# A cross-attention and two-expert feed-forward kernel: the search for the largest expert weights moved from attention into shared-stage tiles 0 to 7, the split of the weights into tiles 8 to 15

## The chip, the cores and the metric

The kernel runs on one core of a Trainium2 chip. The metric is the device time of one execution in microseconds, lower is better. A core has TensorE (PE, matrix products), VectorE (DVE), ScalarE (ACT), GpSimd (POOL) and a queue of its own for loads and stores (SP), which run side by side and wait for one another on semaphores.

## The reference

```python
def reference(x, ctx, tgt_mask, src_mask, ...):          # x 4x1024x512, ctx 4x64x512
    x = x + xattn(layernorm(x), ctx, ...)                # 16 heads of 64, 64 keys, two masks
    return x + ffn(layernorm(x), ...)
def ffn(x, gate_w, w1, b1, w2, b2, sw1, sb1, sw2, sb2):
    top1 = argmax(softmax(xf @ gate_w.T))                # one of two experts for each row
    masked = xf[None] * one_hot(top1).T[:, :, None]      # rows of the other expert are zero
    h = relu(einsum('end,edh->enh', masked, w1) + b1)    # 512 -> 2048
    routing = (einsum('enh,ehd->end', h, w2) + b2).sum(0)
    shared = relu(xf @ sw1 + sb1) @ sw2 + sb2
    return routing + shared
```

A row that an expert isn't given still gets the expert's constant, relu(b1) @ w2 + b2.

## The kernel before

Products are made from float32 in three float16 parts: high times high, high times low, low times high. Each operand is first scaled by a power of two that comes from the largest magnitudes of the weights, and then split into a high half (ScalarE, `eh`) and a low half (VectorE, `el`). So the largest magnitude of a matrix must be known before its first split.

Three stages follow one another, each ended by a barrier of all engines.

**Attention** works on 32 tiles of 128 rows, one an iteration. Each engine has its order written out in `body(g)`: `step(eng, g, u, d, fn)` calls `fn` for the tile `d` ahead of the iteration's. TensorE does transposes (L429, L450), scores (L440) and the output (L461). GpSimd does the two `rstd` chains (L624 to L630), `norm` (L641), `lo_x` (L649), `add_bo` (L645), `sub` (L636) and `low_w` (L658). VectorE does `residual` (L721, L724), `lo_p` (L689), the mask and the statistics (L731, L695), `sums` (L711, L713), the aggregates (L701, L707), `masked` (L737, L742), `gate` (L754), then `largest_w` (L747 twice, L751), and `pick` (L761). `largest_w` reads 128 rows of 512 of `w1` and of `w2` (`ew`, loaded by L377 and L378) and keeps the running maximum `amw`.

**The shared stage** runs all 4096 rows through the shared network: 16 tiles of 256 rows, each in 16 steps `j` over the hidden width. TensorE does `first(j)` (L978, 12 matmuls into `pH`) and then `second(j-2)` (L990, 6 matmuls into `pY`). ScalarE makes the relu twice (L1009, L1011), VectorE takes the low half, `lo_h(j)` (L1024, semaphore `hl`). `second(j)` waits for `hl` of step j, so VectorE's instruction behind a wait holds TensorE up two steps later. At j=3 stands `result` of the tile before (L1032), to which GpSimd adds the bias (L1179), at j=6 four one-hots (L1327, L1328), at j=11 the next tile's `z` (L1017).

Beside this the expert weights go through the core: `load_e` (L1147) fills `er[u]` with 256 rows of `w1` and of `w2` for each tile, `split_hi` and `split_lo` stand at j = 12 and 14 (`BF = 12`), `idle_expert` at j=13 adds relu(b1) times the rows of `w2` to `cacc` (L1366), and `store_e` (L1152, L1153) writes the halves to `e_split`. Before the first split come the maximum over partitions on GpSimd (L1173) and 18 linked steps on VectorE, `expert_scales`, at j=4 of tile 0 (L151 to L172). At tile 1, j=3, VectorE makes `slots()`, a long linked chain for the order of the rows. SP's queue is in order: at the start of the stage it loads the second `z` tile, three quarters of the shared weights, the bias row, then the first x1 rows and the first `er`.

**The expert stage** takes the rows in the order of their experts, 17 tiles, with the split weights read back (L1409, L1410).

`groups(eng, n, body)` writes the iterations -1, 0, 1 and the last ones out and puts the others in a loop of the engine.

## Time and profile before

| | us |
|---|---|
| median of 3 runs (1948.7 to 1955.52) | 1953.84 |
| the profiled execution | 1952.96 |
| its span in the trace | 1951.2 |
| TensorE busy (matmul) | 1881.4 |
| VectorE busy | 855.0 |
| ScalarE busy | 849.4 |
| GpSimd busy | 523.9 |

Attention lasts to about 516 us of the span, the shared stage from 521 to 1220, the expert stage from 1222 to the end. Busy time is an average over stages. What a change is worth is read from the waits: an engine's idle time counts only where TensorE, or the loop that sets an iteration's length, waits for it.

### The profile page before, as it was taken

Reading aid. Unit: us, or ns where it says so; the run is one execution under the profiler, and the core shown is the slowest. Engines: PE = TensorE matmul, PEld = TensorE weight load, DVE = VectorE, ACT = ScalarE, POOL = GpSimd, SP = SyncE. Lnnn points to the kernel's source line nnn. Section 1 sums busy time; section 2 is a strip of 40 time slices with the busy share of each in tenths; the row PEclk is TensorE's granted clock in tenths of the full one; section 3 lists DMA queues with packets and bytes.
Section 4 is the critical chain, followed back from the end, with each engine's and each line's share of the span. In section 5 each row is a group of like instructions: output and inputs, shape, how many; then the busy total and the mean of one; then the engine's idle time right before and its main releaser. Section 6 shows DMA issues by size and latency. Waiting matters only on the chain. (4 is left out here: it accounts for less than half of the span.)

```text
span 1951.2 us, 35601 instructions
## 1 busy us (share of the span) xinstructions
PE 1881.4 (96%) x11964; PEld 1197.9 (61%) x11965; DVE 855.0 (44%) x1669; ACT 849.4 (44%) x1506; POOL 523.9 (27%) x635
## 2 busy tenths in 40 slices
PE   8889999999799999999999999999999999999997
PEld 6344444444466666666666666666666666666664
DVE  6988787778543333333333333222222222222222
ACT  4654444444344444444444443344443343444333
POOL 1068888888300000000000001121221111222111
PEclk9999999999899999999999999999999999999998
DMA  8245555554652222232322261611111010111100
GB/s 318 78 144 176 166 165 167 164 169 153 228 197 77 76 76 76 79 104 75 109 85 75 75 238 65 227 40 38 38 51 33 27 32 29 43 32 47 40 18 15
DMA packets 123587, 197.32 MB, mean 101 GB/s; under 512 B 20208, under 2 KB 61680, under 8 KB 123120
## 3 DMA queue, kind: packets, MB, share of 16 engines
q1 hardware_dynamic: 115584, 171.01, 26.3%
q0 software_dynamic: 7920, 25.17, 4.0%
q8 instruction: 56, 0.92, 0.2%
q14 instruction: 27, 0.22, 0.0%
HBM read 137.95 MB, written 58.98 MB: 101 GB/s over the span
## 5 line engine op out<-in xcount | busy, mean ns | idle before, releaser
L978 PE MATMUL pH<-room_a,room_w 128*128 128x256 f16 (+1 forms) x6336 | 768.6, 272 | 8.2 <-PEq L335 5.3
L990 PE MATMUL pY<-room_w,room_a 128*128 128x512 f16 (+1 forms) x3120 | 757.8, 380 | 4.6 <-DVE room_a L1024 4.6
L978 PEld LDWEIGHTS pH<-room_a,room_w 128*128 (+1 forms) x6336 | 612.1, 98 | 187.8 <-issue 22.0
L1024 DVE TENSOR_TENSOR room_a<-room_a 128x256 f16<-128x256 f32 (+1 forms) x528 | 233.8, 443 | 888.3 <-ACT room_a L1011 888.2
L990 PEld LDWEIGHTS pY<-room_w,room_a 128*128 128x128 f16 x3120 | 305.2, 98 | 264.5 <-DVE room_a L1024 4.9
L1009 ACT ACTIVATE room_a<-pH,e_bsel,sc 128x256 f32<-128x256 f32 (+1 forms) x272 | 151.8, 558 | 406.0 <-PE pH L978 389.7
L1009 ACT ACTIVATE room_a<-pH,b1s,sc 128x256 f32<-128x256 f32 x256 | 144.5, 565 | 365.1 <-PE pH L978 364.4
L1179 POOL TENSOR_TENSOR room_a<-room_a,s_brow 128x512 f32<-128x512 f32 x32 | 42.4, 1348 | 616.6 <-DVE room_a L1032 616.6
L461 PE MATMUL pO<-room_w,room_b 128*128 (+1 forms) x768 | 171.8, 380 | 2.7 <-DVE room_b L689 2.7
L1011 ACT ACTIVATE room_a<-pH,e_bsel,sc 128x256 f16<-128x256 f32 (+1 forms) x272 | 149.6, 550 | 0.0
L1423 POOL DMA_INDIRECT rows_room<-z_scratch,e_iz x33 | 33.7, 1021 | 415.3 <-DVE e_iz L1416 410.1
L1011 ACT ACTIVATE room_a<-pH,b1s,sc 128x256 f16<-128x256 f32 x256 | 142.4, 556 | 0.0
L461 PEld LDWEIGHTS pO<-room_w,room_b 128*128 128x128 f16 x768 | 75.3, 98 | 87.2 <-DVE room_b L689 2.9
L440 PE MATMUL pS<-room_w,room_a 128*128 (+1 forms) x384 | 87.3, 385 | 5.3 <-POOL room_a L649 5.3
L440 PE MATMUL banks_a<-room_w,room_a 128*128 (+1 forms) x384 | 85.6, 379 | 5.4 <-POOL room_a L649 5.2
L1468 POOL TENSOR_TENSOR room_a<-room_a,e_sel 128x512 f32<-128x512 f32 x33 | 43.8, 1347 | 147.8 <-DVE room_a L1032 147.8
L534 ACT ACTIVATE room_b<-room_b,shift,rs 128x512 f32<-128x512 f32 x32 | 26.0, 813 | 117.1 <-POOL shift L630 117.1
L641 POOL TENSOR_TENSOR room_b<-room_b 128x1024 f32<-128x1024 f32 x32 | 71.6, 2237 | 0.0
L440 PEld LDWEIGHTS pS<-room_w,room_a 128*128 128x128 f16 x384 | 37.7, 99 | 50.4 <-issue 7.4
L1017 DVE SCALAR_TENSOR_TENSOR room_a<-banks_a,room_a 128x512 f16<-128x512 f32 x65 | 41.9, 686 | 60.1 <-ACT room_a L999 60.1
L440 PEld LDWEIGHTS banks_a<-room_w,room_a 128*128 128x128 f16 x384 | 37.1, 98 | 50.2 <-issue 4.5
L636 POOL TENSOR_TENSOR room_b<-room_b 128x1024 f32<-128x1024 f32 x32 | 61.3, 1916 | 1.0 <-DVE room_b L742 1.0
(184 smaller groups left out, 1546.7 us busy)
## 6 DMA issues: line engine op xcount, KB each, us to landing
room_b<-in_w SPq DMA_DIRECT2D x64, 256.0 KB, 4.5
s_er<-in_w SPq DMA_DIRECT2D x32, 512.0 KB, 6.3
room_w<-e_split SPq DMA_DIRECT2D x8, 2048.0 KB, 16.8
rows_room<-in_x SPq DMA_DIRECT2D x32, 256.0 KB, 4.6
room_a<-in_sw SPq DMA_DIRECT2D x32, 256.0 KB, 5.0
room_b<-in_x SPq DMA_DIRECT2D x32, 256.0 KB, 2.8
s_split<-room_a SPq DMA_DIRECT2D x64, 128.0 KB, 4.2
x_scratch<-room_b SPq DMA_DIRECT2D x32, 256.0 KB, 3.1
```

Source lines behind the costliest of these rows:

```text
L440: mm = e.matmul(pS[u % 2][:, h * 512:(h + 1) * 512], xt[:, u % 2, k, :], f[:, k, bass.ds(b, 1), h * 512:(h + 1) * 512], start=(n == 0), st ...
L461: mm = e.matmul(pO[:, :], pt[:, q, :], f[:, bass.ds(b, 1), q, :], start=(n == 0), stop=(n == 3 * PAIRS - 1))
L636: e.tensor_tensor(v, v, mx[:, u % 2, :].unsqueeze(2).broadcast_to([P, HEADS, KEYS]), ALU.subtract).then_inc(S["sub"], 1)
L641: e.tensor_tensor(v, v, ri[:, u % 2, :].unsqueeze(2).broadcast_to([P, HEADS, KEYS]), ALU.mult).then_inc(S["prob"], 1)
L978: mm = q.matmul(self.pH[j % 2][:, 0:rows], w[:, k, j * P:(j + 1) * P], zt[:, u, k, 0:rows], start=(n == 0), stop=(n == 3 * KC - 1))
L990: mm = q.matmul(self.pY[u][r][:, :], h[:, j % self.HR, r * P:(r + 1) * P], w[:, j, :], start=(j == 0 and n == 0), stop=(j == HC - 1 and n ...
L1009: q.activation(self.hf[:, j % self.HR, 0:rows], self.pH[j % 2][:, 0:rows], ACT.Relu, bias=b, scale=self.a1)
L1011: q.activation(self.hh[:, j % self.HR, 0:rows], self.pH[j % 2][:, 0:rows], ACT.Relu, bias=b, scale=self.a1).then_inc(self.S["hh"], 1)
L1017: v = q.scalar_tensor_tensor(out=self.zTl[:, u, :, r * P:(r + 1) * P], in0=self.pZ[:, r, :].rearrange("p (k n) -> p k n", k=KC), scalar=LN ...
L1024: q.tensor_tensor(self.hl[:, j % self.HR, 0:rows], self.hf[:, j % self.HR, 0:rows], self.hh[:, j % self.HR, 0:rows], ALU.subtract).then_in ...
L1179: v = q.tensor_tensor(net.ob[:, u, r, :], net.ob[:, u, r, :], brow[:, :], ALU.add)
L1468: v = q.tensor_tensor(net.ob[:, u, r, :], net.ob[:, u, r, :], sel[:, u, :], ALU.add)
```

## The change

In attention, `largest_w`, its two loads an iteration, its buffers and `amw` go.

The shared stage goes over the expert weights twice, in 16 steps each. In tiles 0 to 7, steps 0 to 15, two a tile: VectorE at j=5 and j=12 waits for the load and does `idle_expert`, and in the two `j` behind each takes the largest magnitude of the two halves of `er` (`largest`, one reduce of 1024 elements each, into `seen`). After the last `j` of tile 7 it takes the maximum of `seen`. GpSimd's reduction over partitions and the 18 steps of `expert_scales` move from tile 0 to tile 8 (the latter at j=4 as before). In tiles 8 to 15 the weights are loaded again and split, two steps a tile, at j = 5 and 7 and at j = 12 and 14. SP's order is written anew for this; expert 0's weights are still read back before tile 14's work. SP, GpSimd, ScalarE and VectorE have the stage's iterations all written out (`unrolled`); TensorE keeps its loop and its order. The expert weights are still read from memory twice: 64 loads of 0.25 MB go from attention, and 32 loads of 0.5 MB more stand in the shared stage.

```diff
+def unrolled(n, body):
+    for g in range(-1, n + 1):
+        body(g)
...
-                        def largest_w(e, g, u):
-                            e.wait_ge(S["ew_in", u % 2], 2 * dma_count2(g, u))
-                            for c in range(2):
-                                e.tensor_reduce(ewm[:, u % 2, c:c + 1], ew[:, u % 2, c, :], AX.X, ALU.max,
-                                                apply_absolute_value=True).then_inc(S["ew_max"], 1)
-                            e.wait_ge(S["ew_max"], 2 * count(g, u))
-                            at_least(e, S["amw"], count(g, u) - 1)
-                            e.tensor_tensor(amw[:, 0:2], amw[:, 0:2], ewm[:, u % 2, :], ALU.max).then_inc(S["amw"], 1)
...
-                            at_least(e, S["ew_max"], 2 * count(g, u) - 4)
-                            e.dma_start(ew[:, u % 2, 0, :], rows(units(w1), g, u)).then_inc(S["ew_in", u % 2], 16)
...
-                                step(dve, g, u, 2, largest_w)
...
+        PASS = TILES // 2
+        AT = (5, 12)
...
+                def load_e(q):
+                    if 2 <= q < TILES + 2:
+                        sp.wait_ge(S["seen"], 2 * (q - 1))
+                        sp.wait_ge(S["cacc"], 2 * (q - 1) + 1)
+                    if q >= TILES + 2:
+                        sp.wait_ge(S["el"], 2 * (q - TILES - 1))
+                    for i, w in enumerate((w1, w2)):
+                        sp.dma_start(er[:, q % 2, i, :, :], net.rows(units(w), q % TILES)).then_inc(S[f"e_in{q % 2}"], 16)
+                def store_e(q):
+                    n = q - TILES
+                    sp.wait_ge(S["el"], 2 * n + 2)
+                    for i, d in enumerate((e1_d, e2_d)):
+                        sp.dma_start(net.rows(units(d[0]), n), eh[:, i, :, :]).then_inc(S["e_out"], 16)
...
+                load_z(1)
...
+                load_r(0)
+                load_e(0)
+                for t in range(TILES):
+                    if t > PASS:
+                        store_e(2 * t - 1)
+                    load_e(2 * t + 1)
+                    if t == TILES - 2:
+                        sp.wait_ge(S["e_out"], 64 * TILES // 2)
                         load_set(nc, sp, wB, e1_d, e2_d, 0, w_in)
-                    for u in range(N):
-                        if not isinstance(g, int) or g >= 0:
-                            step(sp, g, u, 2, load_z)
-                        step(sp, g, u, 1, load_r)
-                        step(sp, g, u, 1, load_e)
-                        step(sp, g, u, -1, store)
-                        step(sp, g, u, 0, store_e)
-                groups(sp, TILES // N, body)
+                    if t + 2 < TILES:
+                        load_z(t + 2)
+                    if t + 1 < TILES:
+                        load_r(t + 1)
+                    if t > 0:
+                        store(t - 1)
+                    if t >= PASS:
+                        store_e(2 * t)
+                    if t + 1 < TILES:
+                        load_e(2 * t + 2)
+                store_e(2 * TILES - 1)
+                store(TILES - 1)
...
+                        if N * g + u == PASS:
+                            pool.wait_ge(S["e_am"], 2)
+                            pool.partition_all_reduce(sc[:, ARE:ARE + 3], sc[:, AME:AME + 3], P, RMAX).then_inc(S["e_red"], 1)
...
+                def split_hi(n, i):
+                    act.wait_ge(S[f"e_in{n % 2}"], 16 * TILES + 32 * (n // 2 + 1))
+                    at_least(act, S["e_out"], 64 * n)
+                    act.activation(eh[:, i, :, :], er[:, n % 2, i, :, :], ACT.Copy, scale=sc[:, (EW1, EW2)[i]:(EW1, EW2)[i] + 1]).then_inc(S["eh"], 1)
...
+                            for h, at in enumerate(AT):
+                                if j in (at, at + 2) and PASS <= N * g + u < TILES:
+                                    if N * g + u == PASS and j == AT[0]:
+                                        act.wait_ge(S["e_step"], EXP_STEPS)
+                                    split_hi(2 * (N * g + u - PASS) + h, (j - at) // 2)
...
+                def split_lo(n, i):
+                    dve.wait_ge(S["eh"], 2 * n + i + 1)
+                    dve.scalar_tensor_tensor(out=el[:, i, :, :], in0=er[:, n % 2, i, :, :], scalar=sc[:, (EW1, EW2)[i]:(EW1, EW2)[i] + 1],
+                                             in1=eh[:, i, :, :], op0=ALU.mult, op1=ALU.subtract).then_inc(S["el"], 1)
+                def idle_expert(n):
+                    dve.wait_ge(S[f"e_in{n % 2}"], 32 * (n // 2 + 1))
                     for c in range(2):
-                        q.wait_ge(S["cacc"], 2 * t + c + 1)
-                        e = bass.ds(t // (TILES // 2), 1)
-                        v = cacc[:, e, :].rearrange("p e n -> p (e n)")
-                        q.scalar_tensor_tensor(out=v, in0=er[:, u, 1, c, :], scalar=rb1[:, bass.ds(2 * t + c, 1)], in1=v,
-                                               op0=ALU.mult, op1=ALU.add).then_inc(S["cacc"], 1)
+                        dve.wait_ge(S["cacc"], 2 * n + c + 1)
+                        v = cacc[:, n // PASS, :]
+                        dve.scalar_tensor_tensor(out=v, in0=er[:, n % 2, 1, c, :], scalar=rb1[:, 2 * n + c:2 * n + c + 1], in1=v,
+                                                 op0=ALU.mult, op1=ALU.add).then_inc(S["cacc"], 1)
+                def largest(n, i):
+                    dve.tensor_reduce(seen[:, i, n:n + 1], er[:, n % 2, i, :, :].rearrange("p r n -> p (r n)"), AX.X, ALU.max,
+                                      apply_absolute_value=True).then_inc(S["seen"], 1)
+                def largest_all():
+                    dve.wait_ge(S["seen"], 2 * TILES)
+                    dve.tensor_reduce(sc[:, AME:AME + 2], seen[:, :, :], AX.X, ALU.max).then_inc(S["e_am"], 1)
...
-                            if j == 4 and isinstance(g, int) and g == 0 and u == 0:
+                            if j == 4 and N * g + u == PASS:
...
-                            if j in (BF, BF + 2):
-                                step(dve, g, u, 0, split_lo, (j - BF) // 2)
-                            if j == BF + 1:
-                                step(dve, g, u, 0, idle_expert)
-                dve.tensor_copy(sc[:, AME:AME + 2], amw[:, 0:2])
...
-                groups(dve, TILES // N, body)
+                unrolled(TILES // N, body)
```

VectorE's queue in an iteration of attention, before. The names are buffer<-buffers; L754 is `gate`, L747 and L751 are `largest_w`, L761 `pick`, L721 and L724 `residual`:

```order
L737 SCALAR_TENSOR_TENSOR room_b<-banks_a,sc,room_a 128x1024 [waits a_sim,a_neg]
L742 TENSOR_REDUCE room_b<-room_b 128x16 [waits a_smask]
L754 SCALAR_TENSOR_TENSOR room_a,gg<-room_b,mv,room_a 128x512 [waits a_agg2]
L747 TENSOR_REDUCE room_b<-room_b 128x1 [waits a_ew_in0]
L747 TENSOR_REDUCE room_b<-room_b 128x1
L751 TENSOR_TENSOR amw<-amw,room_b 128x2 [waits a_amw,a_ew_max]
L761 TENSOR_SCALAR expert<-gg,rs 128x1 [waits a_rs2,a_gd]
L721 SCALAR_TENSOR_TENSOR room_b<-pO,sc,room_b 128x512 [waits a_x1_out0,a_z_out0,a_xr_bo,a_att]
L724 BN_STATS st<-room_b 128x6 [waits a_x1]
```

and after, where `gate` is L745 and `pick` L752:

```order
L737 SCALAR_TENSOR_TENSOR room_b<-banks_a,sc,room_a 128x1024 [waits a_sim,a_neg]
L742 TENSOR_REDUCE room_b<-room_b 128x16 [waits a_smask]
L745 SCALAR_TENSOR_TENSOR room_a,gg<-room_b,mv,room_a 128x512 [waits a_agg2]
L752 TENSOR_SCALAR expert<-gg,rs 128x1 [waits a_rs2,a_gd]
L721 SCALAR_TENSOR_TENSOR room_b<-pO,sc,room_b 128x512 [waits a_x1_out0,a_z_out0,a_xr_bo,a_att]
L724 BN_STATS st<-room_b 128x6 [waits a_x1]
```

Nothing else moved; `pick` and `residual` follow `gate` directly.

VectorE's queue at the start of the shared stage, before. L1398 to L1400 stand ahead of tile 0, L1024 is `lo_h`, and with L163 the scales begin:

```order
L1399 TENSOR_SCALAR s_rb<-b1e 128x32
L1400 TENSOR_REDUCE sc<-b1e 128x1
L1024 TENSOR_TENSOR room_a<-room_a 128x256 [waits s_hh,s_rb1]
L1024 TENSOR_TENSOR room_a<-room_a 128x256 [waits s_hh] x4
L163 COPY sc<-sc 128x1 [waits s_e_red]
L151 TENSOR_SCALAR sc<-sc 128x1 [waits s_e_step]
L152 TENSOR_SCALAR sc<-sc 128x1 [waits s_e_step]
L153 TENSOR_SCALAR sc<-sc 128x1 [waits s_e_step]
```

and after, where `lo_h` is L1013, `idle_expert` L1368 and `largest` L1372:

```order
L1414 TENSOR_SCALAR s_rb<-b1e 128x32
L1415 TENSOR_REDUCE sc<-b1e 128x1
L1013 TENSOR_TENSOR room_a<-room_a 128x256 [waits s_hh,s_rb1]
L1013 TENSOR_TENSOR room_a<-room_a 128x256 [waits s_hh] x5
L1368 SCALAR_TENSOR_TENSOR cacc<-s_er,s_rb,cacc 128x512 [waits s_cacc,s_e_in0]
L1368 SCALAR_TENSOR_TENSOR cacc<-s_er,s_rb,cacc 128x512 [waits s_cacc]
L1013 TENSOR_TENSOR room_a<-room_a 128x256 [waits s_hh]
L1372 TENSOR_REDUCE s_seen<-s_er 128x1
```

The scales are gone from here, and the first wait on a load of expert weights (`s_e_in0`) stands behind `lo_h` of j=5.

SP's queue there, before. `room_w<-s_split` are the shared weights, `s_er` the expert weights, `e_split` the stores of their halves:

```order
L1058 DMA room_w<-s_split 128x4x512 x2
L1061 DMA room_w<-s_split 128x4x512 x2
L1137 DMA room_a<-x_scratch 128x2x512 [waits a_x1_out1,a_z_out1,a_z_out0,a_x1_out0]
L1147 DMA s_er<-in_w 128x2x512 x2
L1133 DMA rows_room<-z_scratch 128x2x512 [waits s_zT]
L1137 DMA room_a<-x_scratch 128x2x512
L1147 DMA s_er<-in_w 128x2x512 x2
L1152 DMA e_split<-s_eh 128x2x512 [waits s_el]
L1153 DMA e_split<-s_el 128x2x512
```

and after:

```order
L1047 DMA room_w<-s_split 128x4x512 x2
L1050 DMA room_w<-s_split 128x4x512 x2
L1118 DMA room_a<-x_scratch 128x2x512 [waits a_x1_out1,a_z_out1,a_z_out0,a_x1_out0]
L1132 DMA s_er<-in_w 128x2x512 x4
L1114 DMA rows_room<-z_scratch 128x2x512 [waits s_zT]
L1118 DMA room_a<-x_scratch 128x2x512
L1132 DMA s_er<-in_w 128x2x512 [waits s_cacc,s_seen]
L1132 DMA s_er<-in_w 128x2x512
```

The first load of `er` keeps its place behind the shared weights and the first x1 rows, and the second now follows it at once.

## Rows read from the trace of the kernel before

**Rows 1.** windows of before: stretch, busy us of each engine (instructions), granted clock, DMA

```profile
159.56:485.62 326.06, 313.39 (x1564) 156.37 (x1563) 261.42 (x441) 152.96 (x208) 264.08 (x362) 1.00 0.54 167
...
521.09:564.50 43.41, 43.41 (x298) 30.12 (x299) 15.73 (x43) 19.49 (x36) 1.26 (x3) 0.96 0.73 258
564.50:607.50 43.00, 38.42 (x254) 25.50 (x251) 17.70 (x57) 15.84 (x30) 2.50 (x2) 0.92 0.25 82
```

**Rows 2.** timeline of one attention iteration: start, length, engine, line, [idle before, releaser]

```profile
311.47 0.75 DVE L721 SCALAR_TENSOR_TENSOR room_b<-pO,sc,room_b 128x512 f32<-128x512 f32 x1 [2.47 <-POOL room_b L645]
...
313.03 1.16 POOL L658 TENSOR_TENSOR room_a<-room_a 128x512 f16<-128x512 f32 x1
...
316.37 0.14 DVE L707 BATCH_NORM_AGGREGATE mv<-st 128x2 f32<-128x6 f32 x1
...
318.85 0.74 DVE L754 SCALAR_TENSOR_TENSOR room_a<-room_b,mv,room_a 128x512 f32<-128x512 f32 x1
318.89 2.46 POOL L641 TENSOR_TENSOR room_b<-room_b 128x1024 f32<-128x1024 f32 x1
...
320.83 0.54 DVE L751 TENSOR_TENSOR amw<-amw,room_b 128x2 f32<-128x2 f32 x1
...
321.32 1.15 POOL L649 TENSOR_TENSOR room_a<-room_a 128x512 f16<-128x512 f32 x1
...
322.43 1.27 POOL L645 TENSOR_TENSOR room_b<-room_b,room_a 128x512 f32<-128x512 f32 x1
...
324.00 0.75 DVE L721 SCALAR_TENSOR_TENSOR room_b<-pO,sc,room_b 128x512 f32<-128x512 f32 x1 [2.51 <-POOL room_b L645]
```

**Rows 3.** groups on VectorE, 159 to 480 us: count, busy, mean ns, idle before

```profile
L747 DVE TENSOR_REDUCE room_b<-room_b 128x1 f32<-128x512 f32 x50 | 31.8, 678 | 0.0
...
L721 DVE SCALAR_TENSOR_TENSOR room_b<-pO,sc,room_b 128x512 f32<-128x512 f32 x26 | 19.5, 751 | 61.2 <-POOL room_b L645 35.8 <-issue 25.3
...
L751 DVE TENSOR_TENSOR amw<-amw,room_b 128x2 f32<-128x2 f32 x25 | 14.8, 592 | 0.9
```

**Rows 4.** timeline, TensorE, early attention: the scores of two iterations

```profile
136.22 5.34 PE L440 MATMUL pS<-room_w,room_a 128*128 128x512 f16 x24
...
147.89 5.34 PE L440 MATMUL banks_a<-room_w,room_a 128*128 128x512 f16 x24
```

**Rows 5.** timeline, end of attention: ScalarE, VectorE and GpSimd

```profile
491.12 1.90 POOL L641 TENSOR_TENSOR room_b<-room_b 128x1024 f32<-128x1024 f32 x1
...
496.63 1.02 ACT L522 ACTIVATE room_b<-pP 128x1024 f16<-128x1024 f32 x1 [4.60 <-PE pP L450]
...
498.00 1.21 DVE L689 SCALAR_TENSOR_TENSOR room_b<-pP,room_b 128x1024 f16<-128x1024 f32 x1
```

**Rows 6.** SP's timeline, and issue to landing of its first two `er` loads

```profile
539.34 0.97 SPq L1147 DMA_DIRECT2D s_er<-in_w  x2
...
DMA to landing us min/median/max: 7.0/7.6/8.3
```

**Rows 7.** timeline, tile 0: last of the scale steps, and TensorE's second product j=6

```profile
536.99 0.24 DVE L172 TENSOR_SCALAR b1e_s<-b1e,sc 128x32 f32<-128x32 f32 x1
...
542.49 1.46 PE L990 MATMUL pY<-room_w,room_a 128*128 128x512 f16 x6
```

**Rows 8.** timeline, TensorE, tile 1: the pause and what follows

```profile
585.10 2.74 PE L990 MATMUL pY<-room_w,room_a 128*128 128x512 f16 x6 [4.58 <-DVE room_a L1024]
...
589.98 1.46 PE L990 MATMUL pY<-room_w,room_a 128*128 128x512 f16 x6
```

**Rows 9.** durations: timeline rows of tile 0, and two groups of the whole span

```profile
532.93 0.39 POOL L1173 PARTITION_ALL_REDUCE sc<-sc  x1 [10.97 <-issue]
...
558.51 1.53 DVE L1366 SCALAR_TENSOR_TENSOR cacc<-s_er,s_rb,cacc 128x512 f32<-128x512 f32 x2
...
L770 DVE TENSOR_REDUCE seen<-room_w 128x1 f32<-128x1024 f32 x16 | 19.3, 1209 | 0.0
...
L1328 DVE TENSOR_SCALAR s_hota<-lane,s_place,row_id 128x33 f32<-128x33 f32 x32 | 9.5, 297 | 0.0
```

85 lines of the change are left out of this document (30 added, 55 removed).

## The prediction

> **What bounds the kernel now.** I read it stage by stage. The windows come first [rows 1]: in the 26 attention iterations from 159.56 to 485.62 us TensorE is busy 313.39 of 326.06 us, so it waits about half a microsecond an iteration. In the first shared tile (521.09 to 564.5) it never pauses, 43.41 of 43.41. In the second it pauses 4.58 us. The later shared tiles are like the first. So in the shared stage any other engine's work is free as long as `hl` arrives in time, and everything depends on single waits. In attention, a little could be had.
>
> Then the timeline of one attention iteration [rows 2], to see what sets its length. VectorE adds the residual (L721, 311.47), works without a break to L707 (ends 316.51), and releases GpSimd. GpSimd makes two rstd chains, normalises (L641, 318.89), makes the low part (L649), adds `bo` (L645, ends 323.70) and so releases VectorE's next L721 at 324.00. That loop, 5.0 us on VectorE and 7.2 us on GpSimd with 0.3 us of handing over, is 12.53 us from L721 to L721, and 26 iterations at 12.54 us are the window of [rows 1]. TensorE alone would need 11.67 us: that is the distance of two iterations at the start, before the loop has caught up [rows 4].
>
> **The change, part by part.**
>
> Attention loses `largest_w`: two reduces of 678 ns and a maximum of 592 ns, 1.95 us of VectorE an iteration [rows 3]. They stand after L754 and before L721, that is in VectorE's own time while GpSimd works, not in the loop. In 26 iterations VectorE stood idle 61.2 us before L721, 2.35 each [rows 3]. I expect this idle time to grow to 4.3 us and the iteration to stay at 12.5. The 16.8 MB of loads that go were never waited for. Value taken: 0 for the 26 iterations. At the end of attention there is one place where the three instructions are late work: L689 begins at 498.00, though its input from ScalarE was there at 497.65 [rows 5], so 0.3 us are won; one link of the scales goes at the start, 0.1 us. Term: **-0.4 us**.
>
> The removed maximum has two SBUF inputs and could hold GpSimd. The rows say that it does not: L751 begins at 320.83 and ends with L641 at 321.37, so it waits, and the L649 behind it takes 1.15 us, as L658 does (1.16) with no such instruction beside it [rows 2]. The Trainium skill (SBUF — State Buffer, Who interferes with whom) says that of a VectorE instruction with two SBUF inputs and a GpSimd instruction the one that starts first has the shared ports for its whole length; by that, each of the 25 could have held GpSimd for up to its own length wherever VectorE was first, 25 x 0.59 = 14.8 us to win at most. By the rows here it is nothing.
>
> Tile 0 of the shared stage gains a wait. Before, the first reader of `er` was ScalarE at j=12. Now VectorE waits for `e_in0` at j=5, in `idle_expert`, right behind `lo_h(5)`, with `lo_h(6)` and all later ones queued behind it. Without the 18 steps of the scales, which held it to 537.23 [rows 7], VectorE is there a little earlier still, at about 536.4. But on SP's queue the load of `er` stands behind three quarters of the weights, the bias row and the x1 rows, as before: it is issued at 539.34 in two pieces, which land 7.0 to 8.3 us later [rows 6]. The second goes out at about 539.8, so both are there at 546.8 to 548.1; I take 547.8. Nothing in the change moves this load forward. Behind it come the two multiply-adds, 1.53 us [rows 9], and `lo_h(6)`, 0.43, with 0.15 for hand-overs: `hl(6)` is ready at 549.9. TensorE wants it for the second product at 542.49 [rows 7]. Pause: 549.9 - 542.5 = **+7.4 us** (6.4 to 7.8 by the landings).
>
> After a pause TensorE is slow for a while. The pause of 4.58 us in tile 1 shows the price: one step of six and twelve matmuls took from 585.10 to 589.98, 4.88 us, where 2.60 is usual [rows 8], the granted clock of that stretch being 0.92 [rows 1]. The least is what the six alone lost, 2.74 - 1.46 = 1.3. I take the nearest row whole, **+2.2 us**; a longer pause may cost more, up to one more such step, 4.6.
>
> Tiles 0 to 7: VectorE gets two multiply-adds (1.53 us) and two reduces of 1024 elements (1.21 each [rows 9]) at j=5 to 7 and again at 12 to 14. The worst step is j=6 with the four one-hots (4 x 0.3 [rows 9]): 0.43 + 1.2 + 1.21 = 2.8 us against a step of 2.60, and `hl(j)` is needed two steps after `first(j)`, some 3.5 us after `lo_h` could end. The split of these tiles is gone. 0, in a range to +1. Their loads are issued a tile ahead at j=7 and j=15, with over 20 us to land; SP's order puts no new wait ahead of z, x1 or the stores. 0. Tile 1 keeps the pause of `slots()`, which is unchanged.
>
> Tile 8: the maximum (L1377 in the new file) comes after `lo_h(15)` of tile 7, GpSimd reduces over partitions, and VectorE's 18 steps stand at j=4 of tile 8. That is five steps, 13 us, later. The one such reduction in this stage began 11 us after its operands were there [rows 9] and takes 0.4, so it is in time by about 1.5 us. The 18 steps take at most 3.9 us (533.3, the end of the reduction [rows 9], to 537.23 [rows 7]) and stood at the same j in tile 0 without a pause of TensorE [rows 1]. Here `result` and the bias add of GpSimd stand beside them, which may add 1 us, and the first split follows at once. 0 taken, +2 as the upper end.
>
> Tiles 8 to 15: two steps a tile instead of one, each the pattern that stood at j=12 and 14 and hid completely. Its stores have 12 us until `eh` is written again. At tile 14 they queue behind the 8 MB of expert 0's weights, as no store did at this place before. 0, upper end +2.
>
> Sum, against the profiled execution (1952.96 us, its span 1951.2): 1952.96 - 0.4 + 7.4 + 2.2 = 1962.2. That execution was 0.9 us below the median of the runs, so the forecast is **1963.0 us**. Its own range is 1959 to 1967.
>
> **The rivals.**
>
> Faster. The place is the race in [rows 2]: VectorE's L754 (two SBUF inputs) starts at 318.85, 0.04 us ahead of L641, which then takes 2.46 us; with no such overlap it takes 1.90 (491.12 [rows 5]). L641 is in the loop. If the lighter VectorE queue shifts that order, 0.56 us go in each of some 24 iterations: 13.4 us, and the time is 1963.0 - 13.4 = 1949.6. It decides from a shift of 0.04 us. Against it: nothing that goes stands between L707, which releases both, and L754. The rule of the Trainium skill on that page (who starts first keeps the ports) is what would make such a shift pay. Chance 0.06. The stronger form, that VectorE's queue and not the loop sets the iteration, would bring it to TensorE's 11.67 us: 26 x 0.87 = 22.6 us, 1940.4; the idle 2.35 us before L721 speaks against it. Chance 0.04.
>
> No pause. If the weights landed before 542, or the wait proved harmless, only the -0.4 stays: 1953.4. For it: my landing time rests on two loads. Against: they are issued only at 539.3, and the wait is in VectorE's program order. Chance 0.12.
>
> More pauses. The reduction or the 18 steps are late in tile 8, or the denser splits cost half a microsecond in each of eight tiles: one pause of 2 us with its 2.2 of slow clock, or 8 x 0.5 = 4: 1967 to 1975. For it: the margin at j=5 of tile 8 is of the order of 1 us. Chance 0.13.
>
> The forecast itself has 0.65.
>
> **How the numbers follow.** A measurement of this kernel can tell 0.3%, 5.9 us, from no change; that is 1959.7. The forecast with 0.65 lies above it but for its lower edge, 0.05 (small clock price, early landing); with the more-pauses case, slower is 0.60 + 0.13 = 0.73. Same is 0.05 + 0.12 + half of the first faster case (1949.6 is inside the band), 0.03 = 0.20. Faster is 0.07. The range leaves out the faster cases and the tail of more pauses and takes in the case without a pause: 1953 to 1971.
>
> **What would show it.** Right: in attention L721 still every 12.5 us, with VectorE idle 4.3 us before it; in tile 0 a pause of TensorE near 542 of about 7 us with VectorE's multiply-add on `er` just before its end, released by the load; the shared tiles otherwise at 43 us; at tile 8 no idle TensorE. Wrong: attention's iteration under 12.3 us or L641 at 1.90 throughout; `er` landing before 542; TensorE idle in any of tiles 8 to 15.

## The result, and the profile after

| | before | after |
|---|---|---|
| median of the runs | 1953.88 us (1948.7 to 1955.52) | 1962.63 us (1960.11 to 1967.89) |
| ratio, 95% interval | 1 | 1.0048 (1.0032 to 1.0063) |
| profiled execution: span | 1951.2 us | 1958.4 us |
| first product of the shared stage | 521.09 us | 519.27 us |
| product that opens the expert stage (L1516, now L1531) | 1222.28 us | 1230.45 us |
| length of the shared stage, between the two | 701.19 us | 711.18 us |

The change costs 8.75 us by the medians, 0.4 to 0.5%. The last row says where: the shared stage is 10.0 us longer. Attention ended 1.8 us earlier in this execution, and the expert stage took 1.0 us less (728.9 and 727.95 us from its opening product to the end). Whether these two belong to the change is a question for the runs.

The windows of after, in the stretches of [rows 1] (columns: stretch, then busy us of TensorE, its weight loads, VectorE, ScalarE and GpSimd, granted clock, DMA share, GB/s), and the quiet rest of the stage:

```profile
159.56:485.62 326.06, 312.53 (x1576) 158.51 (x1575) 242.05 (x367) 153.71 (x209) 263.05 (x363) 1.00 0.41 125
521.09:564.50 43.41, 34.83 (x224) 23.05 (x221) 10.02 (x19) 14.33 (x28) 0.00 (x0) 0.86 0.81 269
564.50:607.50 43.00, 38.20 (x258) 25.62 (x257) 23.04 (x63) 13.48 (x27) 2.49 (x2) 0.96 0.27 87
...
607.50:1190.00 582.50, 582.50 (x4073) 400.85 (x4072) 229.57 (x435) 265.55 (x491) 35.20 (x27) 1.00 0.36 123
```

Tile 0, which had no pause before (43.41 of 43.41), has lost 8.58 us. From 607.5 to 1190 us TensorE never pauses: neither the search in tiles 2 to 7, nor the scales in tile 8, nor two splits a tile in tiles 8 to 15 cost anything.

The timeline of after in tile 0, SP's queue, VectorE and TensorE (columns: start us, length us, engine, line, operation; in brackets the idle time before and what ended it). L1132 loads the expert rows, L1368 is the accumulation over the idle expert, L1013 is `lo_h`, L967 and L979 are the first and second products:

```profile
537.89 2.88 SPq L1132 DMA_DIRECT2D s_er<-in_w  x4
547.61 1.54 DVE L1368 SCALAR_TENSOR_TENSOR cacc<-s_er,s_rb,cacc 128x512 f32<-128x512 f32 x2 [12.95 <-DMA s_er<-in_w]
549.07 0.42 DVE L1013 TENSOR_TENSOR room_a<-room_a 128x256 f16<-128x256 f32 x1
549.55 2.74 PE L979 MATMUL pY<-room_w,room_a 128*128 128x512 f16 x6 [8.58 <-DVE room_a L1013]
552.08 2.46 PE L967 MATMUL pH<-room_a,room_w 128*128 128x256 f16 x12
554.37 1.46 PE L979 MATMUL pY<-room_w,room_a 128*128 128x512 f16 x6
```

This is the chain that the prediction drew. VectorE stands 12.95 us for the rows, behind it waits `lo_h(6)`, behind that the second product of j=6. Then one step of eighteen matmuls takes 554.37 - 549.55 = 4.82 us where 2.60 is usual, 2.2 us for the slow clock: the window's granted clock is 0.86, and six matmuls in 2.74 us where 1.46 is usual are near the lower of its two levels, 1.2 of 2.4 GHz.

Tile 8 of after, the scales of the experts (same columns; L1377 is the maximum over the tiles, L1188 the reduction over partitions, L168 and L177 the first and last of the chained steps, L1253 the first split):

```profile
880.08 0.18 DVE L1377 TENSOR_REDUCE sc<-s_seen 128x2 f32<-128x32 f32 x1
880.40 0.39 POOL L1188 PARTITION_ALL_REDUCE sc<-sc  x1 [28.66 <-DVE sc L1377]
893.46 0.14 DVE L168 COPY sc<-sc 128x1 f32<-128x1 f32 x1
896.77 0.24 DVE L177 TENSOR_SCALAR b1e_s<-b1e,sc 128x32 f32<-128x32 f32 x1
897.05 1.15 ACT L1253 ACTIVATE s_eh<-s_er,sc 128x1024 f16<-128x1024 f32 x1 [1.72 <-DVE b1e_s L177]
```

The reduction began 0.1 us after its operands (880.08 + 0.18 to 880.40), and so was ready 12.7 us before it was used. The chain took 3.55 us, and ScalarE waited 1.72 us for it, which nobody felt.

One iteration of attention in after, VectorE and GpSimd, the counterpart of [rows 2] (L745 is `gate`, L754 before; L641 `norm`, L649 `lo_x`, L645 `add_bo`, L721 `residual`):

```profile
319.17 2.48 DVE L745 SCALAR_TENSOR_TENSOR room_a<-room_b,mv,room_a 128x512 f32<-128x512 f32 x1
319.20 1.90 POOL L641 TENSOR_TENSOR room_b<-room_b 128x1024 f32<-128x1024 f32 x1
321.22 1.45 POOL L649 TENSOR_TENSOR room_a<-room_a 128x512 f16<-128x512 f32 x1
322.63 1.27 POOL L645 TENSOR_TENSOR room_b<-room_b,room_a 128x512 f32<-128x512 f32 x1
...
324.20 0.75 DVE L721 SCALAR_TENSOR_TENSOR room_b<-pO,sc,room_b 128x512 f32<-128x512 f32 x1 [2.19 <-POOL room_b L645]
```

This is a surprise. The order of which the faster rival spoke has turned: `gate` starts 0.03 us ahead of `norm`, but is the one that waits (2.48 us where it took 0.74), and `norm` takes 1.90 us where it took 2.46. Yet the iteration is not 0.56 us shorter, only 0.1 (12.39 us from 310.48 to 322.87, where it was 12.50). `gate` ends its work beside `lo_x`, which now takes 1.45 us and not 1.15. From the start of `norm` to the end of `add_bo` it was 4.81 us before (318.89 to 323.70) and is 4.70 now.

So three questions were open. Is tile 0's pause the whole cost? Are the 1.8 us at attention's end a gain of the change? What is the turned order at the port worth?

### The profile page after: what moved, and what is told of

It reads as the page before. It is cut to its first block and busy times, and to the rows that moved or that the text cites. A ratio compares the mean times of both kernels' runs of the same rounds, so it can differ in the third digit from the quotient of the medians.

```text
span 1958.4 us, 34732 instructions
## 1 busy us (share of the span) xinstructions
PE 1880.5 (96%) x11964; PEld 1198.2 (61%) x11965; DVE 861.5 (44%) x1604; ACT 848.2 (43%) x1506; POOL 520.4 (27%) x635
## 5 line engine op out<-in xcount | busy, mean ns | idle before, releaser
L967 PE MATMUL pH<-room_a,room_w 128*128 128x256 f16 (+1 forms) x6336 | 768.8, 272 | 8.3 <-PEq L338 5.3
L979 PE MATMUL pY<-room_w,room_a 128*128 128x512 f16 (+1 forms) x3120 | 758.6, 380 | 13.4 <-DVE room_a L1013 13.4
L967 PEld LDWEIGHTS pH<-room_a,room_w 128*128 (+1 forms) x6336 | 612.4, 98 | 187.7 <-issue 22.6
L1013 DVE TENSOR_TENSOR room_a<-room_a 128x256 f16<-128x256 f32 (+1 forms) x528 | 233.5, 442 | 847.9 <-ACT room_a L1000 842.7
L979 PEld LDWEIGHTS pY<-room_w,room_a 128*128 128x128 f16 x3120 | 305.3, 98 | 273.8 <-DVE room_a L1013 13.9
L461 PE MATMUL pO<-room_w,room_b 128*128 (+1 forms) x768 | 172.7, 382 | 2.6 <-DVE room_b L689 2.6
L461 PEld LDWEIGHTS pO<-room_w,room_b 128*128 128x128 f16 x768 | 75.4, 98 | 87.9 <-DVE room_b L689 3.1
L440 PE MATMUL banks_a<-room_w,room_a 128*128 (+1 forms) x384 | 87.3, 385 | 9.4 <-POOL room_a L649 9.4
L440 PE MATMUL pS<-room_w,room_a 128*128 (+1 forms) x384 | 87.3, 385 | 7.3 <-POOL room_a L649 7.3
L440 PEld LDWEIGHTS banks_a<-room_w,room_a 128*128 128x128 f16 x384 | 37.5, 99 | 55.5 <-issue 8.6
L440 PEld LDWEIGHTS pS<-room_w,room_a 128*128 128x128 f16 x384 | 37.7, 99 | 52.4 <-issue 8.6
L641 POOL TENSOR_TENSOR room_b<-room_b 128x1024 f32<-128x1024 f32 x32 | 63.2, 1976 | 0.0
L721 DVE SCALAR_TENSOR_TENSOR room_b<-pO,sc,room_b 128x512 f32<-128x512 f32 x32 | 24.0, 750 | 86.6 <-POOL room_b L645 78.8
## 6 DMA issues: line engine op xcount, KB each, us to landing
room_w<-e_split SPq DMA_DIRECT2D x8, 2048.0 KB, 18.6
```

Of the source, the lines that this page charges most:

```text
L440: mm = e.matmul(pS[u % 2][:, h * 512:(h + 1) * 512], xt[:, u % 2, k, :], f[:, k, bass.ds(b, 1), h * 512:(h + 1) * 512], start=(n == 0), st ...
L461: mm = e.matmul(pO[:, :], pt[:, q, :], f[:, bass.ds(b, 1), q, :], start=(n == 0), stop=(n == 3 * PAIRS - 1))
L641: e.tensor_tensor(v, v, ri[:, u % 2, :].unsqueeze(2).broadcast_to([P, HEADS, KEYS]), ALU.mult).then_inc(S["prob"], 1)
L967: mm = q.matmul(self.pH[j % 2][:, 0:rows], w[:, k, j * P:(j + 1) * P], zt[:, u, k, 0:rows], start=(n == 0), stop=(n == 3 * KC - 1))
L979: mm = q.matmul(self.pY[u][r][:, :], h[:, j % self.HR, r * P:(r + 1) * P], w[:, j, :], start=(j == 0 and n == 0), stop=(j == HC - 1 and n ...
L1013: q.tensor_tensor(self.hl[:, j % self.HR, 0:rows], self.hf[:, j % self.HR, 0:rows], self.hh[:, j % self.HR, 0:rows], ALU.subtract).then_in ...
```

## The experiments

In all of them the length of the shared stage is measured as in the table above, from its first product to the product that opens the expert stage. It leaves out what attention and the expert stage vary by. Ratios are to the kernel before, run on the same chip in the same rounds. The chips differ: the kernel before took 1950.75 us on that of late_step, early_load, later_load and both_pauses, 1953.54 us on that of attention_only, search_kept, gate_behind and all_three, and 1954.4 us on that of the four repetitions. So an expected time is compared by its ratio.

### Theory and rivals

Theory A: the wait for the expert rows at step 5 of tile 0 makes the whole loss, pause and slow clock. Rival B: the loss lies in the added work of the tiles. If A is right, asking later or loading earlier gives the time back, and loading later costs more.

**late_step.** Tile 0's first search step stands behind step 8 and not step 5:

```diff
+                                    if N * g + u + h == 0:
+                                        at = 8
                                     if j == at:
                                         idle_expert(2 * (N * g + u) + h)
```

> The changed kernel with one edit: in shared-stage tile 0 the first step of the search (the accumulation and the two maxima) stands behind the step 8 in place of step 5 on VectorE; everything else is as changed. Theory A (the pause of tile 0 is what costs): in the changed kernel the accumulation waits until 547.6 us for the expert rows and TensorE stands 8.58 us and then works 2.2 us at the lower clock. Three steps of 1.3 us or more later the pause is gone or is at most 3 us long, and the time falls by 8 to 11 us, from 1962.6 to 1952 to 1955, to about the kernel before. Rival B (the cost is spread over tiles 0 to 15, by the added reductions and the split steps, or lies in the stores): the pause goes and the time stays above 1959. Rival C (the rows are late whenever they are asked for): the accumulation at step 8 still waits more than 5 us and the time stays near 1960.

Measured: 1951.33 us, ratio 1.0004 (0.9995 to 1.0013). The stage took 703.23 us. VectorE and TensorE in its tile 0:

```profile
548.46 1.54 DVE L1368 SCALAR_TENSOR_TENSOR cacc<-s_er,s_rb,cacc 128x512 f32<-128x512 f32 x2 [6.44 <-DMA s_er<-in_w]
550.39 1.47 PE L979 MATMUL pY<-room_w,room_a 128*128 128x512 f16 x6 [2.07 <-DVE room_a L1013]
```

The rows come as late as before, but 7.8 us of TensorE's work (three steps of 2.60) lie ahead of the wait. A pause of 2.07 us is left, and the six matmuls behind it take 1.47 us: no slow clock.

**early_load.** The first pair of expert rows is loaded ahead of the last quarter of the shared weights:

```diff
                 for q in range(1, Q):
+                    if q == Q - 1:
+                        load_e(0)
                     load_quarter(sp, wA, s1_d, s2_d, q, 1, S[f"w1_in{q}"])
...
                 load_r(0)
-                load_e(0)
```

> The changed kernel with one edit: the loads of the first pair of expert rows are issued on SP's queue ahead of the last quarter of the shared weights, at attention's end, and not behind it and the waits for the last stores. Theory A: the rows are there before VectorE's step 5 of tile 0, the 8.58 us pause and its 2.2 us of slow clock go, and the time is 1951 to 1954; the last quarter of the weights lands some 2 to 3 us later and is needed only at step 12 of tile 0, so it costs nothing. Rival B (cost spread over the tiles): above 1959. Rival D (the last quarter comes late in its turn): a new pause in tile 0 at the first matmul of step 12, and 1955 to 1960.

Measured: 1952.1 us, ratio 1.0007 (0.9998 to 1.0016), stage 703.54 us. SP, VectorE and TensorE in its tile 0 (L1369 is the accumulation here):

```profile
530.02 2.37 SPq L1132 DMA_DIRECT2D s_er<-in_w  x2
540.26 1.54 DVE L1369 SCALAR_TENSOR_TENSOR cacc<-s_er,s_rb,cacc 128x512 f32<-128x512 f32 x2 [6.26 <-DMA s_er<-in_w]
542.19 1.47 PE L979 MATMUL pY<-room_w,room_a 128*128 128x512 f16 x6 [1.89 <-DVE room_a L1013]
```

The load goes out 7.9 us earlier and its rows are there 7.3 us earlier. They are still late for step 5, by 1.89 us. The last quarter of the weights was not missed: TensorE has no pause at step 12, the sign of rival D.

**later_load.** The same load, 1 MB later:

```diff
                 load_r(0)
-                load_e(0)
                 for t in range(TILES):
...
+                    if t == 0:
+                        load_z(2)
+                        load_r(1)
+                        load_e(0)
                     load_e(2 * t + 1)
...
```

> The changed kernel with one edit: the first pair of expert rows is loaded behind the z rows of tile 2 and the x1 rows of tile 1 in SP's queue, 1 MB later. Theory A (the pause is as long as the load is late): the pause of 8.58 us grows by the time of 1 MB at the rate of this stretch, about 2.6 us, and the time goes from 1962.6 to about 1965 (1964 to 1967). Rival B (the length of the pause is not what costs): within 1 us of 1962.6.

Measured: 1963.83 us, ratio 1.0067 (1.0053 to 1.0081), stage 714.35 us:

```profile
550.78 1.54 DVE L1371 SCALAR_TENSOR_TENSOR cacc<-s_er,s_rb,cacc 128x512 f32<-128x512 f32 x2 [15.39 <-DMA s_er<-in_w]
552.71 2.74 PE L979 MATMUL pY<-room_w,room_a 128*128 128x512 f16 x6 [11.02 <-DVE room_a L1013]
```

The pause is 11.02 us. Against the three executions with the load unmoved (8.58 above, 7.91 and 9.84 below, mean 8.8) that is 2.2 us more, for a forecast of 2.6. Pause, stage and time move together in all three runs. Theory A stands and rival B has fallen. Rival C was right in one half: at step 8 the accumulation still waited 6.44 us. The time did not stay near 1960 us for that, since the work ahead of the wait covers it.

### Is the gain at attention's end real?

**attention_only.** The kernel before without the search:

```diff
-                            at_least(e, S["ew_max"], 2 * count(g, u) - 4)
-                            e.dma_start(ew[:, u % 2, 0, :], rows(units(w1), g, u)).then_inc(S["ew_in", u % 2], 16)
-                            e.dma_start(ew[:, u % 2, 1, :], rows(units(w2), g, u)).then_inc(S["ew_in", u % 2], 16)
...
-                            link(dve.memset(amw[:, :], 0.0))
+                            link(dve.memset(amw[:, :], 0.1))
...
-                                step(dve, g, u, 2, largest_w)
```

> The kernel before, without the search in attention: its loads of the expert rows (64 in SP's queue) and the step of two maxima and a running maximum are taken out, and the two numbers are a constant 0.1 (the search is left out, so the scales of the expert weights differ; the work of the stages behind does not). The shared stage is that of before. Theory A (as the profile of the changed kernel reads): the attention part is worth 1.8 us to 2.5 us, so 1948.2 to 1949.2 on this chip against 1950.75 of before. Rival as forecast: 0.4 us, so 1950.3. Rival F (the order at the shared port turns and gives the whole 0.56 us to each of the 25 iterations or more): 1937 to 1943.

Measured: 1954.28 us, ratio 1.0002 (0.9993 to 1.0011). Theory A's 1.8 to 2.5 us are refused; the forecast of 0.4 us lies inside the interval, and so does nothing at all. Two groups of its attention, from 160 to 485 us (columns: line, engine, operation, tiles, count, then busy us, mean ns, and idle us before with what ended it; L718 is `residual`, L638 `norm`):

```profile
L718 DVE SCALAR_TENSOR_TENSOR room_b<-pO,sc,room_b 128x512 f32<-128x512 f32 x26 | 19.5, 751 | 104.5 <-POOL room_b L642 104.5
...
L638 POOL TENSOR_TENSOR room_b<-room_b 128x1024 f32<-128x1024 f32 x26 | 60.2, 2315 | 0.0
```

VectorE's idle time before `residual` grew from 61.2 us [rows 3] to 104.5 us, from 2.35 to 4.0 us an iteration. The removed work became waiting, as forecast, and twelve iterations of scores take 150.99 us (311.90 to 462.89) against 150.97 us before (310.17 to 461.14). In this kernel the order at the port has not turned: `norm` takes 2315 ns.

**search_kept.** The changed kernel with the search still in attention, its result unused (the removed loads, `largest_w` and its step put back; shown are the two places that order it):

```diff
                         def load_w(e, g, u):
+                            at_least(e, S["ew_max"], 2 * count(g, u) - 4)
+                            e.dma_start(ew[:, u % 2, 0, :], rows(units(w1), g, u)).then_inc(S["ew_in", u % 2], 16)
+                            e.dma_start(ew[:, u % 2, 1, :], rows(units(w2), g, u)).then_inc(S["ew_in", u % 2], 16)
...
                                 step(dve, g, u, -1, gate)
+                                step(dve, g, u, 2, largest_w)
```

> The changed kernel with the search in attention kept as in before, its result unused: the shared stage is that of the changed kernel, attention that of before. Theory G (the landing of the first expert rows, not attention's end, sets the end of tile 0's pause): attention ends some 1.8 us later, the pause is as much shorter, near 6.8 to 7.4 us, and the time stays that of the changed kernel, within 1 us (ratio to before 1.0048 to 1.0070). Theory H (the rows land as much later as attention ends): the pause stays 8.6 us and the time is 1.8 us above the changed kernel's.

Measured: 1961.8 us, ratio 1.0045 (1.0031 to 1.0059), stage 710.76 us, pause 7.91 us. It is the time of the changed kernel, but it doesn't decide between G and H, since the premise of both failed: with the search kept, the shared stage began at 519.16 us, as early as without it. So the 1.8 us don't come from the search. Nor does the turned order: it stands in this profile too (`gate` 2.48 us beside a `norm` of 1.90 us in two of every four iterations), with the search in place.

**before_again, after_again.** Both kernels unchanged, once more:

> The kernel before, unchanged, once more. Its profiled execution started the shared stage at 521.09 us and the changed kernel's at 519.27 us, while taking the search out of attention alone gave no time (ratio 1.0002) and keeping it gave 519.16 us. Theory L (the start of the stage moves by 1 to 2 us from execution to execution, with where the slow clock falls at attention's end): this profile starts the stage elsewhere than 521.09, between 519 and 523. Theory M (it belongs to the program): 521.1 within 0.3 us. Ratio 1.000 within 0.001.

> The changed kernel, unchanged, once more, on the same chip as the kernels with the pauses taken out. Theory L: the stage starts elsewhere than at 519.27 us, between 519 and 523. Theory M: 519.3 within 0.3 us. The pause of tile 0 is 7.5 to 9 us in either. Ratio to before 1.0048 to 1.0063.

Measured: before 1954.62 us, ratio 1.0001 (0.9992 to 1.001); after 1965.4 us, ratio 1.0054 (1.004 to 1.0068). Before began the shared stage at 522.02 us, after at 522.42 us, 3.1 us later than in its first profile. The end of attention on TensorE in the first profile of after (L461 is the output, L955 the transpose of the first shared rows):

```profile
498.33 7.04 PE L461 MATMUL pO<-room_w,room_b 128*128 128x512 f16 x24 [2.37 <-DVE room_b L689]
...
507.32 1.06 PE L955 MATMUL banks_a<-ident,rows_room 128*128 128x128 f32 x8 [1.07 <-DMA rows_room<-z_scratch]
508.62 5.35 PE L461 MATMUL pO<-room_w,room_b 128*128 128x512 f16 x24 [0.24 <-DVE room_b L689]
519.27 6.07 PE L967 MATMUL pH<-room_a,room_w 128*128 128x256 f16 x36 [5.29 <-PEq L338]
```

and in the second profile of the same kernel:

```profile
499.75 5.35 PE L461 MATMUL pO<-room_w,room_b 128*128 128x512 f16 x24 [2.38 <-DVE room_b L689]
...
509.21 1.91 PE L955 MATMUL banks_a<-ident,rows_room 128*128 128x128 f32 x8 [3.23 <-DMA rows_room<-z_scratch]
510.91 6.22 PE L461 MATMUL pO<-room_w,room_b 128*128 128x512 f16 x24
522.42 5.98 PE L967 MATMUL pH<-room_a,room_w 128*128 128x256 f16 x36 [5.29 <-PEq L338]
```

About 1.7 us of slow clock fall on the last two output products and the transpose between them in both, but at different places. In the first execution the earlier one is slow (7.04 us) and hides in the wait for the shared rows, and the later one runs at full speed (5.35). In the second the earlier is fast, the wait is 3.23 us, and transpose and later product are slow (1.91 and 6.22), in the open. Theory L holds for the changed kernel as far as the start of the stage moves: its two profiles differ by more than the 1.8 us that were to be explained. The kernel before moved by 0.9 us only, with the slow clock in the open both times. What decides where the clock falls, no run tells: the pauses ahead, 2.37 and 2.38 us, are the same. The pause of tile 0, 9.84 us in this second execution, lies above the 7.5 to 9 us that were expected of both.

The place of the slow clock is not all that moved. The order at the port turned in the first profile of after and not in the second, and it can be followed on the scores (L440) from the iteration in which the loop has caught up to the last one, and from there to the first product of the stage:

| | scores, from | to | length | from there to the first product |
|---|---|---|---|---|
| before | 159.56 | 485.19 | 325.63 us | 35.90 us |
| before_again | 160.45 | 486.05 | 325.60 us | 35.97 us |
| after (order turned) | 160.90 | 484.56 | 323.66 us | 34.71 us |
| after_again | 160.28 | 485.98 | 325.70 us | 36.44 us |

Of the 3.1 us between the two executions of after, the turned order has 2.0 and the slow clock 1.7, and the start of the loop takes 0.6 back. The 1.8 us between the first profiles of before and after are 2.0 of the order and 1.2 of the clock, less 1.3 us by which the loop of after began later. Neither can be booked as a gain of the change, since one and the same kernel did it either way. How often each kernel does it, these profiles don't tell.

This pair also gives the cleanest difference, same chip and the same pattern at attention's end: span 1963.2 against 1952.3 us, stage 711.34 against 701.03. The pause of tile 0 in it:

```profile
551.94 1.54 DVE L1368 SCALAR_TENSOR_TENSOR cacc<-s_er,s_rb,cacc 128x512 f32<-128x512 f32 x2 [14.21 <-DMA s_er<-in_w]
...
553.87 2.74 PE L979 MATMUL pY<-room_w,room_a 128*128 128x512 f16 x6 [9.84 <-DVE room_a L1013]
556.40 1.79 PE L967 MATMUL pH<-room_a,room_w 128*128 128x256 f16 x12
558.03 1.46 PE L979 MATMUL pY<-room_w,room_a 128*128 128x512 f16 x6
```

### What is the order at the port worth?

**gate_behind.** In the kernel before, the search's maxima ahead of the gate's product, so that this one can't meet `norm`:

```diff
-                                step(dve, g, u, -1, gate)
                                 step(dve, g, u, 2, largest_w)
+                                step(dve, g, u, -1, gate)
```

> The kernel before with one edit: in attention VectorE does the search's maxima ahead of the gate's product in place of behind it, so that the product no longer starts within 0.05 us of GpSimd's product L641. Nothing is left out. Theory I (the turned order at the port is worth the whole stretch of L641, 2.46 us to 1.90 us, in each iteration): 12.50 us falls to about 11.94 us and the time to 1935 to 1941. Theory J (GpSimd gives the gain back, as in the changed kernel, where L649 went from 1.15 us to 1.45 us and 0.12 us of each iteration was left): 1946 to 1950. Rival K (the product, now late, is itself behind GpSimd and delays the expert's choice): 1950 or slower.

Measured: 1954.19 us, ratio 1.0002 (0.9993 to 1.0011). GpSimd's groups from 160 to 485 us:

```profile
L641 POOL TENSOR_TENSOR room_b<-room_b 128x1024 f32<-128x1024 f32 x26 | 49.5, 1903 | 0.0
L649 POOL TENSOR_TENSOR room_a<-room_a 128x512 f16<-128x512 f32 x26 | 41.1, 1579 | 2.5 <-ACT room_a L517 0.2
```

`norm` fell from 2293 to 1903 ns, `lo_x` rose from 1186 to 1579: what one won, 0.39 us, the other lost. Twelve iterations take 150.90 us against 150.97. Both theory I (0.56 us an iteration) and J's 0.12 us are wrong here; nothing is left. The time is in the range of rival K, but not by its reason: `gate` begins 1.84 us after `norm` and still takes 0.74 us, so it is not held. The collision has only moved from one GpSimd instruction to the next in the same chain.

The shared stage of this kernel, in which nothing was edited, is 1.35 us shorter than before's: about 0.5 us less slow clock at its start, 0.6 us less behind tile 1's pause, and 0.2 us less wait at its end. A difference of that size between two single profiles shows nothing by itself.

### A version that beats both

Tile 1 of both kernels has a pause of its own, 4.58 us before [rows 8] and 4.79 us after: the 35 chained small operations of the slot numbers stand together behind step 3.

**both_pauses**, and again as **two_edits.** The early load, and the slot numbers in pieces of five; `link` now says when a piece is full, and `slots` yields there:

```diff
+                    def link(ins):
+                        issue(ins)
+                        return steps[0] % 5 == 0
...
-                    link(dve.tensor_copy(before, pR[:, 0:SUB]))
+                    if link(dve.tensor_copy(before, pR[:, 0:SUB])):
+                        yield
...
-                            if j == 3 and isinstance(g, int) and g == 0 and u == 1:
-                                slots()
+                            if N * g + u == 0 and j >= 14 or N * g + u == 1 and j < 6:
+                                next(parts, None)
...
```

> The changed kernel with two edits: the early loads as in the kernel before this one, and the 35 chained small operations of the slot numbers, which stood together behind step 3 of tile 1, given in pieces of five behind steps 14 and 15 of tile 0 and 0 to 5 of tile 1. Nothing is left out. Theory A: beside tile 0's pause of 8.58 us and 2.2 us of slow clock, tile 1's pause of 4.6 to 4.8 us and its 2.2 us of slow clock go too; the time is 1943 to 1948, faster than both kernels. Rival E (each piece of about 1.3 us makes VectorE late at its step, seven or eight small pauses): 1949 to 1954, no gain over the early loads alone.

> The kernel with the early loads and the slot numbers in pieces, once more, beside the one with three edits on the same chip. Ratio 0.997 as before.

Measured: 1945.91 us, ratio 0.9975 (0.9966 to 0.9984), stage 694.55 us; again 1947.79 us, ratio 0.9968 (0.9956 to 0.998), stage 694.74 us. The window of tile 1 in two_edits:

```profile
564.50:607.50 43.00, 43.00 (x303) 29.55 (x301) 25.40 (x63) 17.44 (x35) 2.52 (x2) 1.00 0.25 87
```

38.42 busy us at a clock of 0.92 [rows 1] have become 43.00 at 1.00. In tile 0 pauses of 0.82 and 1.28 us are left. This is theory A's range; of rival E's small pauses there is none.

**all_three**, and again as **three_edits.** Both edits, and tile 0's first step behind step 8 as in late_step.

> The changed kernel with three edits: the early loads, the slot numbers in pieces, and the first step of the search in tile 0 behind step 8 in place of step 5. Nothing is left out. With the early loads alone TensorE still stood about 1.7 us in tile 0, since the rows landed at 540.3 us. Theory A: this rest goes too, and the time is 1.5 to 2.0 us below the kernel with two edits (1945.9), near 1944.1. Rival (the search step now falls together with the pieces of the slot numbers and VectorE is late there): 1945.5 to 1948.

> The kernel with three edits once more, on the same chip as the one with two. In the profiles TensorE stood 0.82 us in tile 0 with two edits and not at all with three. If that is what the third is worth, the ratio is 0.0004 below that of two edits, too little to be told from none; if the ratios of the first look (0.9975 and 0.9965) hold, 0.0010 below.

Measured: 1945.86 us, ratio 0.9965 (0.9952 to 0.9979), stage 693.89 us; again 1945.87 us, ratio 0.9959 (0.9945 to 0.9972), stage 693.70 us. From the first product of three_edits on, TensorE does not pause until the end of the stage is near:

```profile
522.53:1190.00 667.47, 667.47 (x4659) 459.48 (x4660) 271.44 (x532) 301.48 (x558) 41.23 (x33) 1.00 0.39 132
```

It is 0.35 to 0.41% faster than the kernel before, and 1.0% faster than the changed one where both ran on one chip (1965.4 to 1945.87). Whether the third edit is worth anything isn't decided. The ratio is 0.0010 and 0.0009 below that of two edits, but the intervals overlap; the stage is 1.0 us shorter, about the pause that went, and less than the 1.35 us by which an unedited stage varied. The rival's late VectorE is not there: TensorE has no pause.

| kernel | pause, tile 0 | stage, us | ratio |
|---|---|---|---|
| before; again | none | 701.19; 701.03 | 1; 1.0001 |
| attention_only | none | 701.35 | 1.0002 |
| gate_behind | none | 699.84 | 1.0002 |
| after; again | 8.58; 9.84 | 711.18; 711.34 | 1.0048; 1.0054 |
| search_kept | 7.91 | 710.76 | 1.0045 |
| later_load | 11.02 | 714.35 | 1.0067 |
| late_step | 2.07 | 703.23 | 1.0004 |
| early_load | 1.89 | 703.54 | 1.0007 |
| both_pauses; two_edits | 0.82; 1.28 | 694.55; 694.74 | 0.9975; 0.9968 |
| all_three; three_edits | none | 693.89; 693.70 | 0.9965; 0.9959 |

## Why the prediction was right, point by point

The time forecast was 1963.0 us and the median is 1962.63 us; the mechanism was the one described. The terms fitted less well than their sum.

**The pause of tile 0, forecast +7.4 us (6.4 to 7.8).** Right in its chain, too short in its length: 7.91, 8.58 and 9.84 us in three executions, all above the range. The step that failed is the landing of the rows. Forecast was 547.8 us, 26.7 us after the stage's first product. Measured from that product it was 27.5 us (search_kept), 28.3 and 29.5 us (after), 29.2 us (late_step). Issuing was later, 18.6 to 19.8 us after the product against 18.25 us before (18.4 in before_again), though the same loads stand ahead of it; no run tells why. And the flight was longer: the forecast took 7.0 to 8.3 us for the pair that is waited for [rows 6], and it took 7.6 to 8.9 us in after, 6.5 to 9.0 us in after_again and 7.1 to 9.5 us in late_step. There four loads go out at once where other rows followed the first two before; whether that made the flight longer, no run separates. By the clock of the trace the forecast landing was nearly met (547.8, measured 547.61), but only because this stage began 1.8 us earlier: TensorE wanted `hl(6)` at 540.97 and not at 542.49, while the rows landed only 0.2 us earlier than forecast. "Nothing in the change moves this load forward" was true. The range was made of the landings of one execution, and was too narrow for that.

**The slow clock behind it, forecast +2.2 us.** Measured 2.2 us (554.37 - 549.55 - 2.60) in after, 1.6 us (558.03 - 553.87 - 2.60) in after_again and 2.5 us in search_kept. The nearest row was the right price for a pause twice as long. It was no matter of length: the 11.02 us of later_load cost 2.6 us, and the 4.6 to 4.8 us of tile 1 cost 1.5 to 2.8 us in the ten profiles that have that pause.

**Attention, forecast -0.4 us.** Not to be told from nothing: attention_only 1.0002 with 0.0009 to either side, search_kept 1.0045 beside the changed kernel's 1.0048. The reasons given hold. The idle time before `residual` grew in the unturned kernels to 4.0 us where 4.3 was said, and the iteration stayed. In the first profile of after it grew only to 2.8 us, as the held `gate` takes part of it. The 0.3 us at the end can even be found: from one output product to the next 8.90 us before (490.37 to 499.27) and 8.59 us in attention_only (492.12 to 500.71). But the wait for the shared rows stands behind them. It was released at 509.21 us in after_again and at 509.08 in before_again, and takes the 0.3 us back.

**Tiles 0 to 7, 8, and 8 to 15: forecast 0.** Right, 582.50 busy of 582.50 us. The margin of tile 8 was thought to be 1.5 us, from the one reduction that had begun 11 us after its operands [rows 9]. It began after 0.1 us here. So the 11 us of that row are no price of the operation; what filled them in before, no run shows.

**The rest.** Tile 1's pause grew from 4.58 to 4.79 us, its clock price fell from 2.3 to 1.7 us (598.88 - 594.59 - 2.60), and the wait for the gathered rows at the end of the stage fell from 1.97 to 1.24 us. With 8.58 and 2.2 that sums to 9.7 of the 10.0 us by which the stage grew; 0.3 us stay unassigned. In the second pair the stage grew by 10.3 us.

**Why the total came out so close.** The stage grew by 10.0 and 10.3 us where 9.6 were forecast (7.4 and 2.2): of the 1.2 to 2.4 us by which the pause was forecast too short, more than half came back in the slow clock and in the waits of the last paragraph. Attention's 0.4 us didn't come. Medians vary more than that from one chip to the next: 1962.63 and 1965.4 us for after, 1950.75 to 1954.4 us for the kernel before. The nearness of 0.4 us is luck; that of 2 us is not.

**The faster rival, 0.56 us in each iteration if the order at the port turned.** The order did turn, in the profiles of after, late_step, early_load, later_load, search_kept and both_pauses, and not in attention_only, all_three, three_edits, two_edits or after_again. It was worth 12.51 us against 12.58 us an iteration (310.48 to 460.65 us in after, 310.98 to 461.92 us in after_again, twelve iterations each), and 2.0 us over the whole loop, where 13.4 us were priced. So the rival's price was wrong, not only its chance, for two reasons. It counted what `norm` wins and not what `lo_x`, next in the same loop, pays (1.15 to 1.45 us). And it counted every iteration, but once the loop has settled the order is open in two of four only: in the third `gate` leads by 0.12 us and kept the port in every profile with this order of the queue, in the fourth it is done before `norm` begins. Had I seen the order turned in the profile and believed the price, I would have looked for 13 us that were never there.

## What to carry to other kernels

When a consumer moves forward on its engine's queue, price the queue of its load too, at the spacing of the new order, and give the landing a range from several executions. Put a first use behind as much of the bottleneck engine's work as the load is late, or split long chains into pieces that fit beside each step; here the early load and the pieces together gave 17.6 us on the chip where both kernels ran (1965.4 to 1947.79). A gain at a shared port counts only when the next instruction in the chain doesn't meet the same rival.
